# Attention on one Trainium2 core: the wait for the bank of the maxima is moved in front of the turned scores of its slot

## What is computed

```python
q, k, v = jnp.split(x @ W_qkv, 3, axis=-1)          # each to (B, 16 heads, T, 16)
attn = jnp.einsum('bhqd,bhkd->bhqk', q, k) * scale
attn = attn + _build_alibi_bias(H, T)               # -slope * |d|, -inf above the diagonal
attn = jax.nn.softmax(attn, axis=-1)
out = jnp.einsum('bhqk,bhkd->bhqd', attn, v)
out = out.transpose(0, 2, 1, 3).reshape(B, T, D)
return out @ W_out
```

## Time and profile before

| what | value |
|---|---|
| median of 3 runs | 4322.66 us (4315.96 to 4324.23) |
| the profiled execution, its own time | 4326.34 us |
| its span, first to last instruction | 4324.6 us |
| mean granted TensorE clock over the span | 0.878 |
| the 30 steps with both passes | 306 to 1317 us of the span |
| one step in the middle of a round of the loop, from its first matmul at 640.91 us to the next one's at 673.63 | 32.72 us |

### The profile page before, as it was taken

How to read it: one execution, slowest core, us unless ns; L and a number is a source line. 1 busy time by engine, 2 the same in 40 slices (tenths; PEclk the granted TensorE clock), 3 DMA queues, 4 the chain that set the end, 5 groups by cost and what they waited for, 6 DMA issues and landing times. The chain is left out here.

```text
span 4324.6 us, 73104 instructions
## 1 busy us (share of the span) xinstructions
PE 3502.0 (81%) x23500; PEld 1669.9 (39%) x23500; DVE 3545.3 (82%) x5194; ACT 2272.3 (53%) x3974; POOL 2379.0 (55%) x1810
## 2 busy tenths in 40 slices
PE   5979999999996699999676777777777777777567
PEld 3634444444443455555322222222222222222156
DVE  4767777777773799999649999998999999999966
ACT  5626666666665233333246566666566565665421
POOL 1100000000000588888448988888888899888823
PEclk8979999999998799999887788888788877888589
DMA  4884445544442111111112222222222222221222
GB/s 146 284 154 65 71 70 76 80 66 71 66 70 53 45 46 46 45 43 39 33 42 61 61 62 50 52 66 68 56 67 64 55 66 63 60 51 43 55 91 81
DMA packets 274031, 300.61 MB, mean 70 GB/s; under 512 B 34559, under 2 KB 204662, under 8 KB 273622
## 3 DMA queue, kind: packets, MB, share of 16 engines
q1 hardware_dynamic: 273630, 295.68, 30.9%
HBM read 210.22 MB, written 84.51 MB: 68 GB/s over the span
## 5 line engine op out<-in xcount | busy, mean ns | idle before, releaser
L1657 POOL TENSOR_TENSOR d_dBu<-d_dtu,d_Bn 128x1024 f32<-128x1024 f32 x512 | 1202.9, 2376 | 157.9 <-DVE d_h L1724 157.8
L756 DVE TENSOR_REDUCE b_Gc<-b_pS 128x1 f32<-128x512 f32 (+4 forms) x1248 | 748.3, 645 | 272.4 <-PE b_pS L647 164.5
L1503 ACT ACTIVATE d_dA<-d_dt,d_decay 128x512 f32<-128x512 f32 x1024 | 688.8, 687 | 432.4 <-DVE d_h L1724 416.5
L729 ACT ACTIVATE b_P<-b_pT 128x512 f32<-128x512 f32 (+1 forms) x1120 | 583.4, 574 | 398.4 <-PE b_pT L635 233.4
L1724 DVE TENSOR_TENSOR_SCAN d_h<-d_dA,d_dBu 128x512 f32<-128x512 f32 x512 | 587.2, 1203 | 60.1 <-ACT d_dA L1503 51.6
L1724 DVE TENSOR_TENSOR_SCAN d_h<-d_dA,d_last_h,d_dBu 128x512 f32<-128x512 f32 x512 | 616.0, 1262 | 18.0 <-ACT d_dA L1503 14.7
L602 POOL CAST b_gp<-b_gT 32x128 bf16<-32x128 f32 x32 | 9.0, 281 | 1054.4 <-ACT b_gT L713 1054.4
L645 PE MATMUL b_pS<-KS,QS 99*128 99x512 bf16 (+3 forms) x1536 | 474.5, 338 | 46.0 <-DVE b_Gc L756 23.7
L633 PE MATMUL b_pT<-QS,KS 102*128 102x512 bf16 (+3 forms) x1536 | 470.6, 330 | 37.5 <-issue 21.1
L1731 DVE TENSOR_TENSOR d_h<-d_h,d_C 128x2048 f32<-128x2048 f32 x192 | 433.7, 2259 | 0.7 <-PE d_C L1386 0.7
L1386 PE MATMUL d_C<-d_bc,d_pick 96*128 96x512 bf16 x256 | 119.5, 467 | 361.3 <-DVE d_h L1731 349.4
(11 more groups left out here) (297 smaller groups left out, 6074.0 us busy)
## 6 DMA issues: line engine op xcount, KB each, us to landing
d_Bn<-scratch_bs SPq DMA_DIRECT2D x64, 1024.0 KB, 8.3
scratch_parts<-a_part SPq DMA_DIRECT2D x48, 512.0 KB, 4.0
QS<-scratch_parts SPq DMA_DIRECT2D x192, 128.0 KB, 6.9
KS<-scratch_parts SPq DMA_DIRECT2D x192, 128.0 KB, 7.1
scratch_v<-a_v SPq DMA_DIRECT2D x16, 1024.0 KB, 7.4
V<-scratch_v SPq DMA_DIRECT2D x32, 512.0 KB, 11.3
a_x<-in_L_attn_x_dram SPq DMA_DIRECT2D x16, 512.0 KB, 7.1
scratch_o<-b_O SPq DMA_DIRECT2D x16, 512.0 KB, 10.3
```

Of the source, the lines that this page charges most:

```text
L729: act.activation(t[:, heads[0]:heads[-1] + 1, c * CH:c * CH + w], pT[:, place % RING, 0:len(heads) * w].rearrange("p (h w) -> p h w", w=w) ...
L756: dve.tensor_reduce(Gc[:, m.k % 2, c, :].rearrange("p (h t) -> p h t", t=QT)[:, heads[0]:heads[-1] + 1, qt], pS[:, j % RING, 0:len(heads) ...
L1503: act.activation(dA[:, m % 2, :], dt[:, c.k % 2, m, :], ACT.Exp, scale=decay[:, m, n:n + 1]).then_inc(dA_d, 1)
L1657: pool.tensor_tensor(dBu[:, n % 2, 2 * j:2 * j + 2, :], dtu[:, c.k % 2, 2 * j:2 * j + 2, :], Bn[:, n // BG % 2, n % BG, :].unsqueeze(1).to ...
```

## The change

The body of `scores` that waits becomes a function of its own, `bank_free`, and the wait for `s_max` goes out of `scores_for_max` to the head of the slot. In a slot with both pieces the order of TensorE's program was: wait `p_done`, turned scores, wait `s_max`, scores for maxima. It becomes: wait `s_max`, wait `p_done` (and `g_ev` where there is one), turned scores, scores for maxima. The turned scores are thus also held until the reduce of slot j - 3 has ended. No matmul, buffer, semaphore or count is changed.

```diff
-            def scores(u, j):
-
-                g, (i, c, heads, w) = u.k % NG, EXPS[j]
-                kt = QT - 1 - i
+            def bank_free(u, j):
+
                 place = j if j < G_AT else j + 1
                 wait(pe, p_done, u.times(NE_, sum((r if r < G_AT else r + 1) <= place - RING for r in range(NE_)) if place >= RING else j - RING + 1))
                 if place == G_AT % RING:
...
                 if place == G_AT + RING:
                     after = 2 if not isinstance(u.base, int) or u.base * NG + u.k + 1 < total else 1
                     wait(pe, g_ev, u.times(1, after))
+
+            def scores(u, j):
+
+                g, (i, c, heads, w) = u.k % NG, EXPS[j]
+                kt = QT - 1 - i
+                place = j if j < G_AT else j + 1
...
                 g, (qt, c, heads, w) = m.k % NG, MAXES[j]
-                wait(pe, s_max, m.times(NM, j - RING + 1))
                 first = qt * P + c * CH
...
+                    if m is not None:
+                        wait(pe, s_max, m.times(NM, j - RING + 1))
                     if u is not None and j < NE_:
+                        bank_free(u, j)
                         scores(u, j)
```

## The result

The changed kernel takes 4338.41 us, median of 6 runs (4336.85 to 4347.73); the median of the kernel before, in its 6 runs, is 4322.53 us. The ratio over all these runs is 1.0045, with a 95% interval of 1.0032 to 1.0059: slower by 0.45%. The two medians alone give 1.0037; two of the six changed runs took more than 4347 us. Forecast were 4335.5 us, 0.30% slower. The profiled execution has a span of 4336.6 us and took 4338.46 us.

The account below looks back on a forecast made before the run. TensorE was taken to bound the attention loop. Moved piece 6.9, dearer release 2.4, slot 0 2.3 and slot 24 1.2 us summed to 12.8 us, taking the median from 4322.66 to 4335.5 us, 0.30% slower; range 4326 to 4346.

Parts of the forecast that it names:

- What bounds: Attention loop: TensorE sets the pace, busy 62.55 of 65 us; its lost time reaches the program unless a later wait returns it.
- the stall of slot 6: TensorE's next stall, waiting for ScalarE's copy; claimed to stay at 0.46 us and not hide the delay.
- The piece in slot 12: Turned piece moves behind the stall, so the maxima piece comes 0.23 us later; 6.9 us in 30 steps.
- The release in slot 12: Two waits start TensorE 0.14 us after release instead of 0.06: 0.08 us extra, 2.4 us in 30 steps.
- Slots 0 and 24: Narrow slots whose turned piece starts late: 0.10 us (2.3 us in 23 steps) and 0.04 us (1.2 us in 30).
- Slot 29: Next narrowest slot after slot 24, with 0.22 us to spare; claimed safe, no cost.
- Slot 6: Slot with three waits, stalled on the last, `g_ev`; nothing taken, other end 0.08 us more, 2.4 us in 30 steps.
- The sum: Whole kernel: 6.9 + 2.4 + 2.3 + 1.2 = 12.8 us, bounds 7.4 and 21.8 us; median 4335.5 us.
- Only the piece moves: Rival: release with two waits costs the same as with one; 7.4 us slower, 4330.1 us; chance 0.17.
- swallowed: Rival: the 0.46 us stall of slot 6 absorbs the delay; time stays 4322.7 us; chance 0.06.
- every slot pays: Rival: turned pieces in the other 35 slots each start 0.05 us late; 52 us, 4388 us; chance 0.04.
- the clock falls: Rival: the longer stall of slot 12 drops TensorE to 1.2 GHz; 62 us on top, 4397 us; chance 0.02.

Follow-up runs that it names:

- e1_slot12: Kernel before, with the wait for the maxima's bank put in front of the turned scores in slot 12 only; ratio 1.0026, 4335.61 us.
- e6_norm6_after: Changed kernel, with VectorE's normalising after the reduce of slot 6 instead of slot 8; ratio to the kernel before 1.0009, 4327.47 us.
- e5_two_more_ahead: Kernel before, with the turned pieces of slots 13 and 14 also issued in slot 12 ahead of the maxima's bank wait; ratio 0.9982, 4316.02 us.
- e3_s_max_last: Changed kernel, with the two front waits swapped: turned scores' bank first, maxima's bank last; ratio to the kernel before 1.0040, 4342.65 us.
- e2_all_but_12: Kernel before, with the wait for the maxima's bank put in front in every slot except slot 12; ratio 1.0012, 4330.80 us.

## Why the prediction was right

*What bounds.* Right: TensorE's lateness in this stage reaches the end of the program. No later stall gave it back; the stall of slot 6 stayed at 0.46 us. One reading beside it was off: the exponential of slot 12 was to come 1.4 us later, while the prediction's own times give 651.70 - 650.46 = 1.24 us. The turned piece did move by 1.24 us, from 9.55 to 10.79 us behind the start of its step, and nothing waited for it.

*The piece in slot 12.* 0.23 us were forecast and 0.23 measured. e1_slot12 shows that this slot alone carries most of the price, e6_norm6_after that it doesn't depend on the length of the stall, and e5_two_more_ahead that it works in the other direction too.

*The release in slot 12.* 0.14 us from the reduce to the matmul were forecast from slot 6, and 0.13 measured, so 0.07 us for this term and not 0.08. The row of another engine's wait was a good stand-in, but not because it too had two waits: e3_s_max_last has as many in slot 12 and starts in 0.06 us. In slot 6 and in slot 12 of the changed kernel alike one instruction of the sequencer lies between the release and the matmul. The prediction counted waits and didn't look at these rows, so that the two places were of one kind was in part luck. The Trainium skill ("Perfetto Trace Analysis", section "Sequencer-only Instruction (DRAIN, etc)") has the wait of such an instruction on the sequencer itself; the trace agrees, with 0.13 us behind one of them and 0.06 us behind none.

*Slots 0 and 24.* 0.10 and 0.04 us forecast, 0.09 and 0.03 measured; e2_all_but_12 has them alone, at 0.13 or 0.14 us a step. Slot 29, with 0.22 us to spare, stayed free.

*Slot 6.* Nothing was forecast, with 0.08 us as the other end, and nothing came. That the other end was real is shown by e3_s_max_last, where it came to 0.10 us.

*The sum.* A step of 33.17 us was forecast and 33.15 measured. The 12.8 us count the stall of slot 12 in 30 steps, and there are 29 of them: 22.9 us by 0.77 us had given 29.7, but step 0 has none. The measured prices make 11.7 us, and the stage grew by 11.6 us in the profile. The size of the whole is less good: the medians differ by 15.9 us, and the lower end of the interval, 0.32%, is 13.8 us. The steps explain 0.27 to 0.30%; the rest, 0.15 points or more of the ratio and 3 to 4 us of the medians, is in no row. The other edits show a surplus of the same sign, so it need not be a cost of this change. Its cause stays open.

*A check that was ill made.* I forecast that the idle time for VectorE in the groups would become 32 us, and it is 27.5. Brackets count from the modelled end of the matmul before, and slots 10 and 11 now start late as well (slot 11 at 650.97, 0.13 us after the reduce of slot 8), which takes a part of the stall ahead of slot 12. The stall as starts show it was larger in both kernels: 1.16 us less the piece of 0.23 is 0.93 us before, against a bracket of 0.77. The distances of starts were the right thing to forecast.

*The rivals.* "Only the piece moves" is out by the 0.13 us; "swallowed" by the 0.46 us that stayed; "every slot pays" by e1_slot12 and e2_all_but_12; "the clock falls" by the 1.00 of the window.

## What to carry to other kernels

In this kernel a wait that was moved ahead of independent work cost that work's length once for each run of slots with a late bank, behind the last of them, and nothing where it was early; the length of the stall didn't enter. Lay the margins out slot by slot (end of the releaser against the start of the piece that will now wait), and count margins below the release time as costs too. When an instruction has several waits, put the one that comes last in time where the fewest of the sequencer's instructions follow it (here 0.06 us with none, 0.13 to 0.14 with one, 0.24 with two), and look into the sequencer's rows for it: being last in the program was enough in slot 12 and not in slot 6. A stall on the engine that bounds is better filled, by issuing independent pieces ahead of the wait, or shortened at its releaser, than made tidy.

## What was not expected of the hardware

The same jump back of the loop costs differently each time. In the profile of the changed kernel TensorE is idle 3.12 us before the first matmul after one jump and then runs at once at full rate (two pieces of 512 columns start 0.22 us apart, the 2.4 GHz level); after 3.26 us at the next jump it runs at the lower level, 1.2 GHz (0.39 us apart), until 612.02, some 6 us. The granted clock was 1.00 in the one stretch and 0.52 in the other (last two lines, columns as in the earlier trace rows):

```profile
469.92 0.39 PE L637 MATMUL b_pT<-QS,KS 102*128 102x512 bf16 x1 [3.12 <-issue]
470.14 0.38 PE L648 MATMUL b_pS<-KS,QS 99*128 99x512 bf16 x1
...
605.96 0.60 PE L637 MATMUL b_pT<-QS,KS 102*128 102x512 bf16 x1 [3.26 <-issue]
606.35 0.63 PE L648 MATMUL b_pS<-KS,QS 99*128 99x512 bf16 x1
...
612.02 0.39 PE L637 MATMUL b_pT<-QS,KS 102*128 102x512 bf16 x1
...
470.00:473.00 3.00, 3.00 (x25) 0.87 (x25) 1.38 (x2) 1.30 (x3) 0.00 (x0) 1.00 0.03 8
606.00:612.00 6.00, 6.00 (x33) 1.39 (x33) 1.66 (x3) 1.79 (x3) 0.00 (x0) 0.52 0.02 4
```

Before, after an idle time of 3.86 us, the first pieces ran at full rate and only later ones slowly. From slot 0 to slot 3 this makes 3.50 us in the one and 6.06 us in the other, where the same stretch in the middle of a round takes 3.50. What the six jumps and the steps behind them add to even steps was between 29.9 us (e2_all_but_12) and 37.3 us (e5_two_more_ahead) over the eleven profiles, and so in the profile of e5_two_more_ahead a gain of 13 us in the steps became 8 us in the stage.
